# The delta stage's slot table laid out anew, and the row sums of the squared outputs taken by ScalarE's accumulator

## What is computed

```python
h = _rmsnorm(x, norm1_w)
q = _l2norm(_short_conv_silu(h @ Wq, conv_q_w)) * dk ** -0.5    # 8 heads of 96
k = _l2norm(_short_conv_silu(h @ Wk, conv_k_w))
v = _short_conv_silu(h @ Wv, conv_v_w)                          # 8 heads of 192
beta = sigmoid(h @ Wb);  g = -exp(A_log) * softplus(h @ Wa + dt_bias)
# over the tokens, per head:
S = S * exp(g_t)
S = S + outer(k_t, (v_t - k_t @ S) * b_t)
o_t = q_t @ S
# after it:
o = _rmsnorm(o, onorm_w) * silu(h @ Wg)
x = x + o @ Wo
```

## Time and profile before

| | |
|---|---|
| median of 3 runs (range) | 3790.98 us (3790.16 to 3799.99) |
| the profiled execution, its span | 3798.17 us, 3795.2 us |
| delta stage in the span | from about 72 to 1638 us |
| busy over the span: PE, DVE, ACT, POOL | 87%, 72%, 54%, 48% |
| mean granted TensorE clock | 0.951 |

### The profile page before, as it was taken

How to read it: one execution, slowest core, us unless ns; L and a number is a source line. 1 busy time by engine, 2 the same in 40 slices (tenths; PEclk the granted TensorE clock), 3 DMA queues, 4 the chain that set the end, 5 groups by cost and what they waited for, 6 DMA issues and landing times. The chain is left out here.

```text
span 3795.2 us, 87218 instructions
## 1 busy us (share of the span) xinstructions
PE 3294.0 (87%) x32714; PEld 2466.9 (65%) x32714; DVE 2723.1 (72%) x5753; ACT 2038.1 (54%) x4599; POOL 1804.8 (48%) x1647
## 2 busy tenths in 40 slices
PE   4789999999999999968999999986898599899998
PEld 3577777777777777745666566654666366656665
DVE  5577777777777777647777677775999477767775
ACT  3456565656565656513666366632444366636662
POOL 3355555555555555434666166632122466526662
PEclk8689999999999999989999999997999799999999
DMA  4111111111111111033122321222112222131122
GB/s 123 23 24 25 25 25 25 26 25 26 24 27 24 27 25 24 11 95 81 43 53 56 93 50 44 71 79 55 47 50 55 63 49 64 45 95 44 46 71 70
DMA packets 409630, 182.71 MB, mean 48 GB/s; under 512 B 235808, under 2 KB 384384, under 8 KB 406656
## 3 DMA queue, kind: packets, MB, share of 16 engines
q1 hardware_dynamic: 409216, 177.15, 19.0%
HBM read 94.47 MB, written 40.12 MB: 35 GB/s over the span
## 5 line engine op out<-in xcount | busy, mean ns | idle before, releaser
L1197 POOL TENSOR_TENSOR delta_cv<-delta_cv,delta_last_tap 96x256 f32<-96x256 f32 (+1 forms) x384 | 332.7, 867 | 623.4 <-DVE delta_cv L1631 623.4
L1938 POOL TENSOR_TENSOR g_a_rn<-g_a_clip,g_minus_half 128x16 f32<-128x16 f32 x64 | 186.4, 2912 | 271.2 <-DVE g_a_clip L2202 243.0
L1938 POOL TENSOR_TENSOR f_a_rn<-f_a_clip,f_minus_half 128x16 f32<-128x16 f32 x64 | 186.3, 2911 | 260.7 <-DVE f_a_clip L2202 232.5
L2155 ACT ACTIVATE g_a_pr<-g_ps,g_a_nb,g_a_rn 128x128 f32<-128x128 f32 x512 | 185.5, 468 | 146.4 <-DVE g_a_nb L2236 146.4
L2155 ACT ACTIVATE f_a_pr<-f_ps,f_a_nb,f_a_rn 128x128 f32<-128x128 f32 x512 | 185.5, 468 | 146.4 <-DVE f_a_nb L2236 146.4
L1466 ACT ACTIVATE delta_cv<-delta_ps,delta_conv_qk 96x256 f32<-96x256 f32 x256 | 120.9, 472 | 253.5 <-PE delta_ps L1299 252.7
L1623 DVE SCALAR_TENSOR_TENSOR delta_cv<-delta_ps,delta_conv_qk,delta_cv 96x256 f32<-96x256 f32 x256 | 122.1, 477 | 169.5 <-ACT delta_last_tap L1468 169.2
L1243 PE MATMUL delta_ps<-delta_state,delta_qk 96*128 96x192 f32 x1024 | 199.4, 339 | 27.3 <-issue 22.8
L1623 DVE SCALAR_TENSOR_TENSOR delta_cv<-delta_ps,delta_conv_v,delta_cv 128x256 f32<-128x256 f32 x192 | 92.1, 480 | 155.5 <-ACT delta_last_tap L1468 154.1
L1243 PEld LDWEIGHTS delta_ps<-delta_state,delta_qk 96*128 96x128 f32 x1024 | 168.3, 193 | 41.7 <-issue 38.1
L1466 ACT ACTIVATE delta_cv<-delta_ps,delta_conv_v 128x256 f32<-128x256 f32 x192 | 90.5, 471 | 127.5 <-PE delta_ps L1299 127.5
(11 more groups left out here) (350 smaller groups left out, 10477.3 us busy)
## 6 DMA issues: line engine op xcount, KB each, us to landing
f_a_vm<-f_a_v SPq DMA_DIRECT2D x128, 130.0 KB, 2.3
g_a_vm<-g_a_v SPq DMA_DIRECT2D x128, 130.0 KB, 2.3
delta_gd<-delta_dram_row SPq DMA_DIRECT2D x16, 1024.0 KB, 4.6
window_vm<-window_v SPq DMA_DIRECT2D x64, 128.0 KB, 2.3
f_m_x<-y SPq DMA_DIRECT2D x24, 256.0 KB, 3.5
delta_dram_inv<-delta_sub SPq DMA_DIRECT2D x16, 256.0 KB, 2.1
f_m_more<-x SPq DMA_DIRECT2D x16, 256.0 KB, 3.9
x<-f_m_x SPq DMA_DIRECT2D x16, 256.0 KB, 2.3
```

Source lines behind the costliest of these rows:

```text
L1197: pool.tensor_tensor(cv[0:M, t % 3], cv[0:M, t % 3], last_tap[0:M, t % 3], ALU.add).then_inc(summed.sem, 1)
L1938: pool.tensor_tensor(rn[:, u % 2], clip[:, u % 2], minus_half[:], ALU.pow).then_inc(rn_sb.sem, 1)
L2155: e = act.activation(pr[:, u % 2, half, i, :], ps[:, score_bank(u, half), i * P:(i + 1) * P], ACT.Exp, bias=nb[:, u % 2, half, i:i + 1], s ...
```

## The change

Nothing is computed otherwise than before, up to the order of some sums.

- **The table.** The first pair of scans goes to slots 24 and 25 of the unit before (-4, -3), the second pair to 8 and 9. `kq`'s second pair goes from 17, 18 to 18, 20, and `load_decays`, bound to it, from 19 to 21. The gate projections, which were at chunk slots 2, 2, 5, go to 6, 10, 11 of even chunks and 2, 7, 11 of odd ones (unit slots 12, 16, 17 and 22, 27, 31). `ot` goes from 21, 22, 25 to 19, 22, 23. `y` is cut into three sums of 4 blocks at 25, 26, 27, each added by VectorE. `vt` and the last `y6` move by a slot here and there, and VectorE's transposes of `tt` come one slot after the `y4` they stood behind.
- **GpSimd and the rates.** `rn` is one power of 16 columns in slot 15; `of` goes from chunk slot 12 to 14, ahead of the multiplication by the gate; `diagonal_rates` goes from slot 16 to 15, and the betas are loaded ahead of the squares. `q_eps` goes from chunk slot 3 to 6.
- **The row sums.** ScalarE squares o head by head (8 instructions of 192 columns for 2 of 768, chunk slots 12, 13) and writes each head's sum through its accumulator output; VectorE's two reductions go.

```diff
@@ the table of slots
 
     K_NORM = 15
     SOLVE_AT = 16
-    KK_AT, KQ_AT = ((6, 7), (9, 10)), ((13, 14), (17, 18))
-    INVERT_AT = dict(x4=23, y4=25, x5=28, y5=30, x6=32, y6=34)
-    GATE_AT, OT_AT, Y_AT = (2, 2, 5), (21, 22, 25), 27
+    SCAN_AT = ((-4, -3), (8, 9))
+    KK_AT, KQ_AT = ((6, 7), (9, 10)), ((13, 14), (18, 20))
+    VT_AT = ((20, 21), (23, 24), (26, 28), (29, 30))
+    INVERT_AT = dict(x4=(23, 24), y4=(25, 26), x5=(28, 29), y5=(30, 31), x6=(32, 33), y6=(34, 36))
+    TURN_AT = (26, 27)
+    GATE_AT, OT_AT, Y_AT = ((6, 10, 11), (2, 7, 11)), (19, 22, 23), (25, 26, 27)
+
+    def scanned(t, cc, i):
+
+        when = SCAN_AT[i][cc]
+        if when < 0 and t < SLOTS + when:
+            return 0 if t == cc else None
+        return unit(t, when)
...
@@ SyncE
-                n = unit(t, 31)
+                n = unit(t, START + HALF + GATE_AT[1][2] - SLOTS + 1)
                 if n is not None and n + 2 < UNITS:
                     take(sp, ("gate", 2 * n - 1, 2))
                     load_ht(n + 2)
...
                 n = unit(t, KQ_AT[1][1] + 1)
                 if n is not None and n + 1 < UNITS:
...
                     sp.dma_start(sub[:, 0], diag_d.rearrange("b c h j i -> (b c h) j i")).then_inc(diag_in.sem, 16)
+                    betas = row_d[1, 2 * H * n:2 * H * (n + 1), :].rearrange("r (b i) -> b r i", i=16)
+                    sp.dma_start(sub_beta[:], betas).then_inc(beta_in.sem, 16)
                     brk_sb.need(sp, n - 1)
                     for b in range(B16):
                         squares = diag_d[b].rearrange("c h j i -> (j i) (c h)")[0:256:17, :]
                         sp.dma_start(n2k[16 * b:16 * b + 16, :], squares, allow_slow_non_contiguous=True).then_inc(n2k_in.sem, 16)
-                    betas = row_d[1, 2 * H * n:2 * H * (n + 1), :].rearrange("r (b i) -> b r i", i=16)
-                    sp.dma_start(sub_beta[:], betas).then_inc(beta_in.sem, 16)
...
@@ GpSimd
-                for cc in range(2):
-                    n = unit(t, K_NORM + cc)
-                    if n is not None:
-                        ins = pool.tensor_tensor(rn[:, n % 2, cols(cc)], n2[:, n % 2, cols(cc)], minus_half[:, 0:H], ALU.pow)
-                        if cc == 1:
-                            ins.then_inc(rn_sb.sem, 1)
-                n = unit(t, K_NORM + 6)
+                    pool.tensor_tensor(rn[:, n % 2], n2[:, n % 2], minus_half[:], ALU.pow).then_inc(rn_sb.sem, 1)
+                n = unit(t, K_NORM + 7)
...
+                C = chunk(t, 14)
+                if C is not None:
+                    ostat_sb.need(pool, C)
+                    o_normed.need(pool, C - 1)
+                    pool.tensor_tensor(of[:], ostat[:, 1, :], minus_half[:, 0:H], ALU.pow).then_inc(of_sb.sem, 1)
                 for i in range(2):
                     C = chunk(t, 14 + i)
...
-                C = chunk(t, 12)
-                if C is not None:
-                    ostat_step.need(pool, C)
-                    o_normed.need(pool, C - 1)
-                    pool.tensor_tensor(of[:], ostat[:, 1, :], minus_half[:, 0:H], ALU.pow).then_inc(of_sb.sem, 1)
...
@@ TensorE
-                C = chunk(t, Y_AT)
-                if C is not None:
-                    copied(pe, ("ot", C, 2))
-                    bank = claim(pe, ("y", C))
-                    for m in range(NV):
-                        mm = pe.matmul(ps[:, bank, 0:D], ot[:, m, :], wo[:, m, :], start=m == 0, stop=m == NV - 1)
-                    filled(mm, ("y", C))
+                for k, when in enumerate(Y_AT):
+                    C = chunk(t, when)
+                    if C is not None:
+                        copied(pe, ("ot", C, k))
+                        bank = claim(pe, ("y", C, k))
+                        for m in range(4 * k, 4 * k + 4):
+                            mm = pe.matmul(ps[:, bank, 0:D], ot[:, m, :], wo[:, m, :], start=m == 4 * k, stop=m == 4 * k + 3)
+                        filled(mm, ("y", C, k))
...
@@ ScalarE
-                C = chunk(t, 10 + i)
+                C = chunk(t, 12 + i)
                 if C is not None:
                     o_sb.need(act, C, i + 1)
                     up_ps.need(act, C, i + 1)
-                    mine = slice(HB * i, HB * i + HB)
-                    act.activation(vr[:, C % 3, mine], o[:, C % 2, mine], ACT.Square).then_inc(osq_sb.sem, 1)
+                    of_sb.need(act, C - 1)
+                    for h in heads(i):
+                        e = act.activation(vr[:, C % 3, h, :], o[:, C % 2, h, :], ACT.Square, accum_out=ostat[:, 0, h:h + 1])
+                    e.then_inc(osq_sb.sem, 1)
...
@@ VectorE
-                C = chunk(t, 3)
+                C = chunk(t, 6)
                 if C is not None:
                     q_summed.need(dve, C)
-                    ostat_step.need(dve, C - 2)
+                    ostat_sb.need(dve, C - 2)
                     dve.tensor_scalar(q_eps[:, C % 2], q_sum[:, C % 2], 1e-6 * DK, 1e-12 * DK, ALU.mult, ALU.add)\
                         .then_inc(q_eps_sb.sem, 1)
-                for i in range(2):
-                    C = chunk(t, 11 + i)
-                    if C is not None:
-                        osq_sb.need(dve, C, i + 1)
-                        mine = slice(HB * i, HB * i + HB)
-                        dve.tensor_reduce(ostat[:, 0, mine], vr[:, C % 3, mine], AX.X, ALU.add).then_inc(ostat_step.sem, 1)
-                C = chunk(t, 12)
+                C = chunk(t, 13)
...
-                C = chunk(t, Y_AT)
-                if C is not None:
-                    y_in[C % 2].need(dve, C // 2)
-                    stored[C % 2].need(dve, C // 2 - 1)
-                    bank = take(dve, ("y", C))
-                    emptied(dve.tensor_tensor(out[:, C % 2], ps[:, bank, 0:D], yres[:, C % 2], ALU.add), ("y", C))
+                for k, when in enumerate(Y_AT):
+                    C = chunk(t, when)
+                    if C is not None:
+                        if k == 0:
+                            y_in[C % 2].need(dve, C // 2)
+                            stored[C % 2].need(dve, C // 2 - 1)
+                        else:
+                            copied(dve, ("y", C, k - 1))
+                        bank = take(dve, ("y", C, k))
+                        emptied(dve.tensor_tensor(out[:, C % 2], ps[:, bank, 0:D], (yres if k == 0 else out)[:, C % 2], ALU.add),
+                                ("y", C, k))
                 for cc in range(2):
                     for i in range(2):
                         mine = slice(HB * i, HB * i + HB)
-                        n = unit(t, 2 * cc + i)
+                        n = scanned(t, cc, i)
                         if n is not None:
                             dec_in.need(dve, n)
...
             def diagonal_rates(t):
-                n = unit(t, SOLVE_AT)
+                n = unit(t, SOLVE_AT - 1)
```

97 lines of the change are left out of this document (51 added, 46 removed).

## The result

| | before | after |
|---|---|---|
| median (range), same chip | 3795.48 us (3790.16 to 3802.89) | 3845.57 us (3838.57 to 3849.16) |
| ratio, 95% interval | | 1.013 [1.011, 1.015] |
| profiled execution, span | 3798.17, 3795.2 us | 3847.97, 3846.2 us |
| mean granted TensorE clock | 0.951 | 0.948 |

The changed kernel is 50 us slower where 33 us less were forecast, and outside the range given. The page's first line says little by itself: VectorE and GpSimd have less to do than in the earlier trace rows and ScalarE more. TensorE has the same number of matmuls and is busy for 21.3 us more; the span is 51.0 us longer, so the other 29.7 us are idle time of TensorE.

What follows compares the result with a forecast made beforehand. It took TensorE's order of work as the frame, some 8.9 us idle per unit. A unit was 44.0 + 44.2 + 3.5 for the clock = 91.7 against 93.9 us; over 15 units 33 us less, 3758, range 3690 to 3820.

Steps and rivals of the forecast that it cites:

- The four waits named: TensorE's waits per unit: 2.7 us before a gate projection, 1.6 before the state products, 0.8 and 0.7 in the inversion; all go.
- The hold: Slot 25: TensorE, 6 us early, waits before its first `y4` until 44.0 us, because the decays load behind the inverse.
- first `y4` after the last `kk`: First part of a unit, ended by the late decays, slot 24's scan and `x4`: 44.0 us, against 45.9 before.
- VectorE's lateness in slots 6 to 10: Two scans there, beside fewer gate projections on TensorE, make the last `kk` about 1.6 us later against TensorE.
- port 0: Scans in slots 8, 9 beside GpSimd's multiplications: no delay in the sum, since `q_eps` leaves; +1.8 us per unit for the range.
- the chain gives 1.2 of it back: VectorE's slot 15 is closer to the late `kk`, so 1.2 of the 1.6 us returns, net +0.4.
- steps that were given no wait: First `y4` to next last `kk`: 45.7 us, less 1.5 for the inversion's waits and 0.4 for a moved `ot`.
- clock: TensorE's low clock per unit: 1.3 us behind the wait at slot 25 plus 2.2 for every second unit, together 3.5.
- the drop of every second unit: TensorE's low clock after the inversion's waits in alternate units, left as it is: a mean of 2.2 us per unit.
- The clock turns it round: Rival: after slot 25's wait TensorE runs at 1.2 GHz, 4.5 us instead of 1.3; 15 us slower, 3806; chance 0.24.
- Nothing comes of it: Rival: the wait at slot 25, ports and clock return what was gained; within 11 us of 3791; chance 0.16.
- The full gain: Rival: the decays land in time, no wait at slot 25; units of 86.5 us, 111 us gained, 3680; chance 0.1.

## Why the prediction was wrong

**What held.** The four waits named went. The chain from `kk` to the inverse's store is 27.3 to 27.5 us (27.5 forecast), which is in part luck: with the second scans early it is 27.9, and the late `kk`, counted by the forecast in another term, takes 0.6 off. The hold is where it was said to be, at `y4`, through the scan of slot 24 and the bank of `x4`. Four squares with their sums keep ScalarE for 1.4 us (1.5), and no wait of TensorE in the list goes back to them: the one nearest in place, for ScalarE's `o` before the state products, is 15.9 us with the accumulator and 16.2 in the run without it. `q_eps` is 0.16 us.

**What failed, in the order of the sum.** A unit was to take 91.7 us and took 97.6:

| step as the prediction put it | forecast | measured | off by |
|---|---|---|---|
| first `y4` after the last `kk` | 44.0 | 45.2 | +1.2 |
| VectorE's lateness in slots 6 to 10 ("some 2 us of scans beside 2 us less of gate projections", 1.6; port 0) | +1.6 | +3.4 | +1.8 |
| "since VectorE's slot 15 is then that much closer, the chain gives 1.2 of it back" | -1.2 | 0 | +1.2 |
| steps that were given no wait (second part without clock and scans) | 43.8 | 46.1 | +2.3 |
| clock | +3.5 | +3.0 | -0.5 |

These sum to 6.0, and the units show 5.9.

- *First `y4`*: the chain of 27.3 to 27.5 is right. SyncE needed 10.4 to 12.2 us to the decays' issue, 11.0 on average, not 10.3, and the landing took 4.9 instead of 4.6. Of the wait of 6 us only a part became one: TensorE was not there 37.9 us after `kk` but some 43, since it had stood on the way, in the unit shown for 1.5 us before `x4`, whose bank a gate still held, 1.2 before the state products, 1.1 before a transpose of v, 0.9 before a `kq`, and 1.1 in small waits. So the hold measured 2 us a unit.
- *The port*: the measured excess over the forecast's 1.6 is the 1.8 us that I kept for the range, and that is luck too: I had taken one whole multiplication, 1.8 us, as the most that a scan can lose, and one scan lost 2.5 (3.73 for 1.21) while the other lost nothing. The place of the error is the reason given for the 0, that `q_eps` leaves slot 9: what counts is not what left, but that the scan stands beside two multiplications and a tap of GpSimd. The Trainium skill's rule ("SBUF — State Buffer", section "SBUF: two separate sides") spoke against the change and was nearer, with a gain of 6 us instead of 33. The trace agrees with it in that both engines are held by turns (1.57 for 0.72, 3.73 for 1.21). It goes beyond it in that the waiting scan was passed by GpSimd instructions issued after it.
- *What the chain gives back*: I had fixed the first part by the chain, at 27.5 us counted from the `kk`, and took 1.2 off on top of that. The measured 45.2 holds already what came back, so the term stands at 0 in the table. What came back is 0.7 us with the hold, nearly all in the chain to the inverse (27.9 to 27.3), and 1.7 without it. The 1.2 assumed that all of VectorE's lateness but 0.4 is made up.
- *New waits*: six rows in the list of waits after, of which I had foreseen one. I had taken for each step moved whether its old wait goes, and not whether its new slot has room. `of` "goes behind it", 1.65 us into slots 20 and 34, was counted in the solve's favour and nowhere against the multiplication by the gate; on the kernel before that costs 40 us, on the change with early scans 30.
- *Clock*: the sum is nearly right by luck, and its parts are not. I had 1.3 for the hold and 2.2 for the drop of every second unit; the hold alone costs 3.0, and the regular drop of the earlier trace rows is gone: no second part of the kernel after has a low stretch other than the one behind `y4`.

**The rivals.** "The clock turns it round" named the mechanism that is there, 8 us at 0.52 to 0.79 behind a wait of 1.4 to 3.1 us, but it decides from 5.7 us a unit and is 3.0. "Nothing comes of it" had the terms (hold, ports, clock) and stopped at zero. The loss is these terms at their measured size, together with the waits that no case had. The full gain was never near: with no hold and no scan beside a multiplication, the new table gives 3764, and 3733 with `of` moved; the 3680 assumed that waits which go aren't replaced.

## What to carry to other kernels

A unit whose period is held by one chain of fixed length (store, load, solve, load) gives nothing for waits taken away ahead of that chain: two edits here (the accumulator alone, `of` on the change) only made the wait at its end longer, and a third, which changed the order within it (the decays first), handed the wait to the next load; and in this kernel each wait before `y4` of 1.4 to 3.1 us was followed by 3 to 10 us at 1.2 GHz. So first ask of each candidate whether the work that ends the chain is started earlier, and change two places of a table singly as well as together, because their costs need not add up: 32 and 21 us made 82 here. When a step is moved, cost its new neighbours on every queue that it enters: on GpSimd, what stands behind it, and on VectorE, which GpSimd instructions run beside it.

## What the hardware showed that I had not expected

- A VectorE scan of 128x512 (1.21 us) that began inside a GpSimd multiplication took 3.73 us, until GpSimd's tap and next multiplication, which followed without a gap, were done as well. The scan of the slot before, begun while GpSimd was idle, took 1.21 us, and made the tap beside it take 1.57 instead of 0.72.
- ScalarE's accumulator output is a second instruction, 191 ns, which overlaps the next square: 0.35 us per square of 192 columns, four with their sums 1.38 us to ScalarE's next work.
- In the kernel after, each wait of TensorE before `y4` (1.4 to 3.1 us) was followed by 3 to 10 us at a granted clock of 0.50, that is 1.2 GHz. The length of the wait decided neither whether that came nor how long it lasted: there, 1.74 us was followed by some 10 us and 1.75 by some 3; with the scans in 24,25 / 4,5, 1.04 us was followed by 0.71 over 5 us, and 1.13 by 1.00. What else decides was not tried.
